# Half the space for the descriptors of GpSimd's transfers, in a Mamba-2 layer with a mixture of experts on one core

## The reference

```python
xn = _layernorm(x, axis=-1)
x = x + _L0_attn_ref(xn, ...) + _L0_ffn_ref(xn, ...)

# _L0_attn_ref: normalise, project to z, x, B, C and dt, convolve over 4 tokens, SiLU,
Y_diag = jnp.einsum('bcln,bcsn,bhcls,bcshp->bclhp', Cc, Bc, Lmat, Xc)
states = jnp.einsum('bcln,bhcl,bclhp->bchpn', Bc, decay_states, Xc)   # then a scan over chunks
Y_off = jnp.einsum('bcln,bchpn,bhcl->bclhp', Cc, states_prev, state_decay_out)
y = (Y_diag + Y_off + xs * D) * silu(z)
y = y * jax.lax.rsqrt(jnp.mean(y * y, -1, keepdims=True) + EPS) * rms_w
return x + y @ W_out.T

# _L0_ffn_ref: the two likeliest of 8 experts for each token, weighted
weights_BTX, indices_BTX = jax.lax.top_k(probs_BTE, 2)
fuse = jax.nn.silu(x @ gating[e]) * (x @ up[e])
out = sum over e of (fuse @ down[e]) * full_weights[e]
```

## Time and profile before

| | us |
|---|---|
| single runs | 787.53, 794.13, 796.54 |
| median of the runs | 794.13 |
| the profiled execution | 795.79 |
| its span (first to last instruction) | 794.0 |
| mean granted TensorE clock in it | 0.938 of full speed |

### The profile page before, as it was taken

One profiled execution on the slowest core, in us unless ns is written; L12 is line 12 of the kernel. 1 busy time (PEld: TensorE's weight loads), 2 busy tenths in 40 slices (PEclk: granted clock), 3 DMA queues, 4 the chain that ended last, 5 costly groups with the idle time before them and its releaser, 6 DMA issues. The chain is left out here.

```text
span 794.0 us, 15139 instructions
## 1 busy us (share of the span) xinstructions
PE 631.2 (79%) x3701; PEld 531.9 (67%) x3703; DVE 585.2 (74%) x1410; ACT 462.3 (58%) x1014; POOL 400.4 (50%) x601
## 2 busy tenths in 40 slices
PE   0695629998999989999998998699898889988700
PEld 0695317777778777778777776587777777777600
DVE  7787898898898888888898888555565555654445
ACT  0352446688777878877788775454555555554400
POOL 3000006576766766766676767145555555555510
PEclk9999999799999999999999999799999999999955
DMA  9950100000000000000000015133333333333169
GB/s 306 266 130 0 29 1 23 19 27 23 29 22 22 28 22 22 28 22 22 25 26 22 29 24 184 36 88 99 97 85 96 88 98 98 85 98 86 54 252 382
DMA packets 64647, 61.43 MB, mean 77 GB/s; under 512 B 9242, under 2 KB 55710, under 8 KB 64624
## 3 DMA queue, kind: packets, MB, share of 16 engines
q1 hardware_dynamic: 56176, 44.11, 19.7%
q0 software_dynamic: 8448, 17.06, 6.2%
HBM read 30.19 MB, written 31.47 MB: 78 GB/s over the span
## 5 line engine op out<-in xcount | busy, mean ns | idle before, releaser
L449 POOL DMA_INDIRECT moe_d<-raw,slot_st x136 | 133.8, 984 | 124.6 <-issue 102.1
L422 POOL DMA_INDIRECT slots_d<-rows,slot_st x128 | 134.6, 1052 | 73.8 <-POOL rows L417 52.5
L1040 DVE SCALAR_TENSOR_TENSOR act<-raw,taps,act 128x512 f32<-128x512 f32 x192 | 149.3, 785 | 23.9 <-ACT act L513 23.1
L398 POOL TENSOR_TENSOR xde<-xb,e_end 128x256 f32<-128x256 f32 x64 | 45.6, 713 | 113.2 <-DVE xb L1117 111.6
L1233 DVE CAST x_hi<-bank 128x256 fp32r<-128x256 f32 x68 | 28.8, 424 | 95.4 <-PE bank L871 91.8
L864 PE MATMUL bank<-xw_hi,x_hi 128*128 x136 | 61.1, 449 | 27.2 <-DVE x_lo L1235 22.7
L774 PE MATMUL bank<-xb,m_sb 128*128 128x64 f32 x512 | 75.9, 298 | 3.8 <-POOL xde L398 3.8
L774 PEld LDWEIGHTS bank<-xb,m_sb 128*128 128x128 f32 x512 | 73.1, 216 | 5.6 <-issue 3.9
L890 PE MATMUL bank<-act,raw 128*128 x544 | 72.0, 275 | 1.8 <-issue 1.8
L664 ACT ACTIVATE raw<-bank 128x256 f32<-128x256 f32 x68 | 26.5, 391 | 77.2 <-remote 68.5
L890 PEld LDWEIGHTS bank<-act,raw 128*128 128x128 f32 x544 | 66.1, 192 | 1.9 <-issue 1.9
(11 more groups left out here) (231 smaller groups left out, 1659.4 us busy)
## 6 DMA issues: line engine op xcount, KB each, us to landing
slots_d<-rows SPq DMA_DIRECT2D x8, 1122.0 KB, 13.4
rows<-slots_d SPq DMA_DIRECT2D x68, 132.0 KB
x_sb<-in_x SPq DMA_DIRECT2D x8, 512.0 KB, 7.0
act<-in_x SPq DMA_DIRECT2D x64, 64.0 KB
xw_hi<-moe_d SPq DMA_DIRECT2D x8, 512.0 KB, 9.3
xw_lo<-moe_d SPq DMA_DIRECT2D x8, 512.0 KB, 9.9
out<-x_sb SPq DMA_DIRECT2D x8, 512.0 KB, 13.5
moe_d<-raw,slot_st POOLq DMA_INDIRECT x136
```

The lines of the kernel that those rows point to most:

```text
L398: nc.gpsimd.tensor_tensor(by_head(xde[:, u, :]), by_head(xdt[:, u, :]), per_head(e_end, nn), ALU.mult).then_inc(xde_done, 1)
L422: nc.gpsimd.indirect_dma_start(out=slots_d, out_offset=bass.IndirectOffsetOnAxis(ap=slot_st[:, r, c:c + 1], axis=0), in_=rows[:, r, c, :], ...
L449: nc.gpsimd.indirect_dma_start(out=moe_d, out_offset=bass.IndirectOffsetOnAxis(ap=slot_st[:, r, c:c + 1], axis=0), in_=ym[r][:, c * D:(c + ...
L1040: V.scalar_tensor_tensor(out=group_act(par)[:, t, :], in0=proj[:, t, k:k + GT], scalar=taps[:, t, k:k + 1], in1=group_act(par)[:, t, :], o ...
```

## The change

The program object is made with 8,192 bytes of each partition for the descriptors in place of 16,384:

```diff
-    nc = bacc.Bacc("TRN2", target_bir_lowering=False, num_devices=1)
+    nc = bacc.Bacc("TRN2", target_bir_lowering=False, num_devices=1, dynamic_dma_scratch_size=8192)
```

## The result

| | before | after |
|---|---|---|
| median of the runs, us | 793.92 (787.53 to 796.54, 4 runs) | 802.39 (800.79 to 803.82, 4 runs) |
| the profiled execution, us | 795.79 | 802.47 |
| its span, us | 794.0 | 800.7 |
| mean granted TensorE clock | 0.938 | 0.937 |

The changed kernel takes 1.0123 of the time of before, 95% interval 1.0089 to 1.0158. That is 8.5 us slower, where 1.1 us was forecast, and it lies above the range.

A forecast was written before the change was run, and what follows sets the result against it. No engine was seen as always busy (PE 79%, DVE 74%, POOL 50%); descriptor space mattered only through scatter rows and waits. Row 0, loop wait 0, experts' wait 1.1, placement 0: +1.1 us, 794.13 to 795.2 us, range 788.5 to 800.5.

The forecast's parts named there:

- The row of a scatter is unchanged: POOL's scatter rows, both stages: still 984 ns with the experts and 1,052 in the loop; effect 0.
- The first wait comes after half as many scatters, at 57: GpSimd's waits for descriptor space: the first, at scatter 114 with the whole space, comes at 57 with half.
- Four waits, one more with the experts: GpSimd's scatters: four waits for space in place of two, one more in the loop and one more with the experts.
- one every 64 in place of 128: Spacing of GpSimd's waits: one every 64 scatters in place of 128, if the space sets the distance.
- A wait in the loop over sequences costs nothing: Loop over sequences: an added wait for space costs 0, with bounds of 0 and 1.8 us.
- A wait with the experts costs 1.1 us: Experts' stage: one more wait for space adds 1.1 us, with bounds of 0 and 1.9 us.
- Ahead of the first scatter of a four the idle time covers a wait: Experts' stage: a wait on a group's first scatter costs 0, since 2.2 us of idle time cover the landing.
- The place in SBUF: Tensors lie 8,192 bytes lower: taken as 0; as a rival, a side effect either way, 790 or 798 us, chance 0.05.
- The range: Whole kernel, 788.5 to 800.5 us: the sum's ends, half the run spread, and 1.8 us for an uncovered loop wait.
- far more waits: Rival: half the space holds far fewer scatters, kernel over 1% slower; 812 us or more at one every 8; chance 0.05.

The follow-up runs named there:

- the third set: One chip: kernel before 792.84 us; 18,432 bytes for descriptors 788.89, with three GpSimd delays 798.08, with 15 delays 806.91; the changed kernel (8,192 bytes) 797.81.
- the `pad`: Changed kernel (8,192 bytes) plus an unused 8,192-byte tensor ahead of all others, keeping every tensor in its old place: 803.28 us, ratio 1.0108 to before.
- the first set: Beside before at 796.63 us: 8,192 bytes with old places 803.28; 4,096 bytes with old places 802.4; 18,432 bytes 792.69; 16,384 bytes with `rows`, `slot_st` first 797.67.
- the repeat of the third: The changed kernel (8,192 bytes) run again beside the 18,432-byte kernels, on a chip where before takes 792.84 us: 797.81 us, ratio 1.0072 to before.

## Why the prediction was wrong

- *The row of a scatter is unchanged*: right (984, 1,052 to 1,056 ns). What GpSimd makes in such a row no run shows.
- *The first wait comes after half as many scatters, at 57*: right, and the series of sizes bears it out. With 4,096, 8,192, 12,288, 16,384 and 18,432 bytes the first wait is at 29, 57, 86, 114 and 128. An estimate from these five: if a scatter takes a fixed part of the space, and the first to wait is the first that finds too little left, then 8,192 bytes hold 56 scatters and not 57, so one takes 143.7 to 146.3 bytes. The 12,288 bytes, which hold 85, put it at 144.6 at most, and the 18,432 bytes, which do not hold 128, at more than 144.0; between these two all five sizes agree. What a scatter puts there no run shows.
- *Four waits, one more with the experts*: wrong. There were five, and three with the experts. The second came 50 after the first, not 57 or 64 (22 after it at 4 KiB), as if six scatters' space were not to be had again. With the experts the series starts anew: 185 = 128 + 57 and 235 = 128 + 107, as 242 = 128 + 114 before. So the 128 between the two waits of before was not the distance from wait to wait, but the place at which the second series began. The reading "one every 64 in place of 128" stood on two waits and could not tell this. The count is not complete either: 157 = 107 + 50 goes on with the old series, and at 4 KiB two of the places it gives are plain rows.
- *A wait in the loop over sequences costs nothing*: right. The stage of the experts starts at 519.79 in place of 520.12, and TensorE waits for `xde` 3.7 us after, 3.8 us before. The reason given was wrong in part: a first scatter of a tile was to have nothing to wait for, since the scatter ahead of it had long landed. It waits all the same, by 1.28 us.
- *A wait with the experts costs 1.1 us*: this is the step that failed. Two more waits at 1.1 us would have been 2.2 us, still within 1%. On the chips where before takes 793 to 797 us one costs about 3 in the mean: 8.9 us for three in the third set. In single profiles it is anything from under 1 us to 7. The 1.1 itself was read too low, from a stretch of 26 us. It was set against 14 x 1.7625 = 24.68 us, the pace of the middle of the stage, but without the wait (18,432 bytes) the same 14 scatters take 23.78, so 2.0 us were lost in that stretch and 0.9 behind its end: 2.9 us. The lower clock of the last 39 us, 0.88, is no sign of the wait: it is 0.87 in the same window without it, since TensorE's work ends within these 39 us. Over the whole kernel before is slower than with 18,432 bytes by 796.63 - 792.69 = 3.9, 792.84 - 788.89 = 4.0 and 794.38 - 788.69 = 5.7 us in three sets, in which the waits at 114, 128 and 256 differ too (the tensors lie 2 KiB apart as well, but 4,256 bytes had no effect). The two waits more then cost 8.5 us in the first result, 6.7 with the `pad` in the first set and 5.0 in the repeat of the third: 2.5 to 4.2 each. What the price left out is what follows: sixes, pauses and pairs in all engines until the fours are back.
- *Ahead of the first scatter of a four the idle time covers a wait*: wrong. At 235, the first of a four, the idle time is 3.43 us in the changed kernel, 3.50 in the kernel with `pad` and 3.41 in the repeat of the third set, where 2.2 is usual: the wait comes on top. The 2.2 us of idle time are no slack: in them GpSimd waits for results that TensorE, ScalarE and VectorE are making. The scatter of rows 6 at 570.52 starts 0.14 us behind the end of VectorE's `slot_st` (L1241, 570.22 + 0.16 = 570.38, timeline of before). That the row behind gets longer because the next pair's results have come in the meantime fits the rows, but no run tests it. Which place in a four is the dearest stays open: delays between pairs cost 3.6 us and inside a pair 1.8, but the wait at 242, the second of an undisturbed four, cost 2.9.
- *The place in SBUF*: right, 0 (ratio 1.0006).
- *The range*: its upper end had one price for one wait in the loop, where nothing was lost, and none for another price with the experts. The rival of "far more waits" asked for eight more at 1.1 us to reach 1%; two more with the experts did it in the first result. In the repeats of the changed kernel the ratio was 1.0072 and 1.0056, under 1%, and still several times the 1.1 us.

The account is not closed. That other engines stand still until about the landing of the last scatter is seen in the rows on these chips, and not on the one where before takes 765 us. What holds TensorE's results back there is open; no run varied it. So the runs show that a late GpSimd is enough for the loss, and the rows show how it spreads, but not why the other engines stop. Also open is why the series starts anew with the experts, and what takes the space of six scatters.

## What to carry to other kernels

Here a wait was priced by what the engines do until the old order is back, not by how long it holds its own engine (a delay of 1.8 us between two pairs cost 3.6): follow the timeline past it until the groups have their old length, and compare with a kernel that has no wait at all. Idle time ahead of an engine's group of instructions is no cover when the engine is waiting there for results that keep coming (2.2 us here, and 3.4 to 3.5 with a wait for space). For GpSimd's transfers, count the scatters of a phase against the space for descriptors, and try a size with which the wait falls at the phase's end: 18,432 bytes, the one such size that was run, were measured at 0.9933 to 0.9969 of before, in three sets. 12,288 bytes gave 0.9965 on the chip where before takes 765 us, against the expectation, so the rule is not the whole story.

## What was not expected of the hardware

- A scatter that waits for space costs GpSimd time even when the one before it should have landed: 0.62 us more at 4 KiB and 1.28 at 8 KiB in the loop, with the last scatter's start 4.5 to 7.6 us back, where one landed 2.09 us behind its start. Twice the space took about twice the time there; with the experts, 8 KiB shows both 0.5 to 0.6 us (157) and 1.2 to 1.3 (235).
- While scatters follow each other 0.3 us apart, results of TensorE's rows reach VectorE late: 3.8 us with six in a row (above), 1.19 with four, where the transposes end at 610.13 + 0.38 = 610.51 (timeline of before, PE and DVE, below). On the chip where before takes 765 us it is 0.04 us. The experts' stage takes 207 to 208 us in the three profiles of that chip that have the scatters, and 232 to 250 us in all others; the times of before differ by 28 to 32 us.
- Less space was not worse: 4 KiB cost 5.8 us where 8 KiB cost 6.7 in the same set, which the intervals can't tell apart.

```profile
610.13 0.38 PE L871 MATMUL bank<-ident,rows 128*128 128x128 f32 x2
...
611.70 0.42 DVE L1233 CAST x_hi<-bank 128x256 fp32r<-128x256 f32 x1 [2.10 <-PE bank L871]
```

`x_hi` is free to start at 610.51 by its input and starts 1.19 us later, 2.07 us behind the start of the last scatter of its four (609.63).
